# One-core adaptive-norm transformer block: last orthogonalisation moved ahead of one feed-forward batch, and the dense products of the block solve spread between the small ones

## The chip, the core and the metric

The program runs on one core of one Trainium2 chip. TensorE (PE) multiplies into eight PSUM banks, ScalarE (ACT) empties the banks, VectorE (DVE) does reductions and elementwise work, GpSimd (POOL) takes a few powers, SyncE (SP) issues the DMAs. The metric is the device time of one execution in microseconds; lower is better.

## The reference

For each of 16 batches of 512 tokens with 128 features: a modulated layer norm, then a chunked ridge attention with 16 heads of 64 features in four chunks of 128 tokens, then a second modulated layer norm and a feed-forward layer whose operands are rounded to a four-bit grid in blocks of 16.

```python
def step(S, qkv):
    Qc, Kc, Vc = qkv
    G = Kc.T @ Kc + RIDGE_EPS * I
    W = jnp.linalg.solve(G, Kc.T @ Vc)
    U = U0
    for _ in range(POWER_K):
        U, _ = jnp.linalg.qr(W @ U)
    Wr = U @ (U.T @ W)
    S_new = DECAY_ALPHA * S + Wr
    return (S_new, SCALE * (Qc @ S_new))
...
gate = fp4_linear(x, w_gate)
y = fp4_linear(x, w_up)
h = jax.nn.silu(gate) * y
return fp4_linear(h, w_down)
```

## The kernel before

The batches are taken in four groups (g = 0 to 3) of four. A group has 256 small systems of size 64 (16 chunks times 16 heads). Each 64x64 Gram matrix is inverted by halves of 32: `lead_extract` turns the leading 32x32 blocks so that VectorE can factor 256 of them at once (`factor`, called by `lead(g)`); `schur(g)` forms the Schur complement on TensorE, VectorE factors that too (`schur(g)` of the vector program), and `assemble(g)` puts the inverse together. `subspace(g)` then applies the inverses in the power iteration, VectorE orthogonalises the eight basis vectors (`orthogonalise(g)`), and `output(g)` and `write(g)` make the attention output.

TensorE's `schur` and `assemble` share one inner scheme, called **a solve stage** here. It runs over four parts k of 64 systems. `scale_rows(k)` is 64 small products (32x32 weights, 64 columns, line 697) into two banks. `squares(k)` takes four banks: first four dense products, called **masks** here (128x128 weights, 256 columns, line 707), which put the known half of the result into each bank, and then 64 small products (line 713) that add the squares of the scaled rows. The order is scale(0), scale(1), masks(0) and squares(0), scale(2), masks(1) and squares(1), scale(3), masks(2) and squares(2), masks(3) and squares(3). A float32 product is two matmul records in the profile, each with a weight load of its own, so one stage has 1056 matmul records: 1024 small and 32 dense.

All engines work in the order in which their instructions are written. TensorE and ScalarE run the same list of steps: a step of TensorE fills banks in turn, the same step of ScalarE empties them. `straight` runs steps one after another; `woven` interleaves two lists by the share of their banks that is done. A `yield` in a step is a place where `woven` may change lists.

In the main loop, for g = 0 to 2, the order on TensorE is assemble(g) (woven with write(g-1) where there is one), subspace(g), lead_return(g+1), schur(g+1), then output(g) woven with the next group's Gram stage. VectorE's order is schur(g), lead(g+1), one weight quantisation, orthogonalise(g), schur(g+1). schur(0) is woven with the fronts (the first layer norms) of batches 8 to 15.

The last group (`last_group`, line 1273) is woven with the feed-forward batches. A batch b has three steps on TensorE and ScalarE: `g` (transposes of the hidden input, then eight products with the gate and up weights), `t` (transposes of the quantised hidden layer) and `y` (down projection, residual). The list `steps` says in which order, `begin` and `wait` cut it: the steps up to `begin` are woven with subspace(3), those up to `wait` follow straight, the others up to batch 7 are woven with output(3) and write(3), which begins by waiting for VectorE's orthogonalise(3) (line 867). On VectorE `quantise(b)` stands between g(b) and t(b); it waits for ScalarE's flag `gate_ok`. ScalarE in turn empties g(b)'s products only when quantise(b-1) has read the ones before (line 953, `hh_ok`). `tile_hat(n)` (steps `n`) is ScalarE's normalisation of a group of four batches, `hidden.stats` and `hidden.finish` are VectorE's parts of the same.

Of the kernel before, what the change touches and what calls it, by code (L numbers as in the profile page):

```python
# [41 lines left out]
DH = 64  # L42
# [14 lines left out]
GB_N = 4  # L57
G = B // GB_N
T = GB_N * NC
HB = 32  # L60
# [222 lines left out]
NQ = T * HP  # L283
# [45 lines left out]
def main_pass(nc, x, ln_g, ln_b, c, wmod, Wq, Wk, Wv, Wo, w_gate, w_up, w_down, s_mod, s_c, s_xnt, s_base, s_x1, out):  # L329


    with ExitStack() as ctx:
# [145 lines left out]
        class Tensor:  # L478
# [211 lines left out]
            def scale_rows(self, k, stationary, moving):  # L690

                two = self.u.fill(2, apart=True)
                for i in range(8):
                    for c in range(4):
                        for s in range(2):
                            q = 32 * k + 8 * c + i
                            last = nc.tensor.matmul(two[s][HB * c:HB * c + HB, i * DH:(i + 1) * DH], stationary(s, q), moving(s, q),  # L697
                                                    start=True, stop=True)
                last.then_inc(filled, 2)
                return self.u.mark()  # L700

            def squares(self, k, half, mask, known):

                four = self.u.fill(4, apart=True)
                for c in range(4):
                    at = 32 * k + 8 * c
                    nc.tensor.matmul(four[c][:].rearrange("p (q z c) -> p q z c", z=2, c=HB)[:, :, half], mask[:], known[:, at:at + 8, :],  # L707
                                     start=True, stop=False, skip_group_check=True)
                for i in range(8):
                    for c in range(4):  # L710
                        for s in range(2):
                            both = scaled[HB * c:HB * c + HB, (2 * k + s) * 8 + i, :]
                            last = nc.tensor.matmul(four[c][rows(s, None), i * DH:(i + 1) * DH], both, both, start=False, stop=True,  # L713
                                                    skip_group_check=True)
                last.then_inc(filled, 4)
                return self.u.mark()

            def schur(self, g):
# [4 lines left out]

                def scale(k):
                    return self.scale_rows(k, lambda s, q: work[rows(s, 0), q, :],
                                           lambda s, q: beside(eyes[0][rows(s, 0)], gram[rows(s, 0), q, :]))

                marks = [scale(0)]
                yield
                for k in range(NQ // 32):  # L730
                    if k + 1 < NQ // 32:
                        marks.append(scale(k + 1))
                        yield
                    self.u.need(marks[k], apart=True)
                    m = self.squares(k, 1, minus[1], gram)
                    yield
                yield from self.to_problems(gram, m)

            def assemble(self, g):
# [6 lines left out]

                def scale(k):
                    return self.scale_rows(k, lambda s, q: work[rows(s, 1), q, :],
                                           lambda s, q: beside(kept[rows(s, 1), q, :], eyes[1][rows(s, 1)]))

                marks = [scale(0)]
                yield
                for k in range(NQ // 32):
                    if k + 1 < NQ // 32:
                        marks.append(scale(k + 1))
                        yield
                    self.u.need(marks[k], apart=True)
                    self.squares(k, 0, minus[0], kept)
                    yield
# [163 lines left out]
        class Scalar:  # L923
# [177 lines left out]
            def solved(self, dst, scale=1.0):  # L1101
                self.scale_rows(0)
                yield
                for k in range(NQ // 32):
                    if k + 1 < NQ // 32:
                        self.scale_rows(k + 1)
                        yield
# [656 lines left out]
```

## Time and profile before

| | us |
|---|---|
| median of three executions | 1335.05 (1333.93 to 1336.13) |
| the profiled execution | 1337.31 |
| its span, first to last instruction | 1335.5 |

| engine | busy us | share of the span | instructions |
|---|---|---|---|
| TensorE, matmul | 989.9 | 74% | 17632 |
| TensorE, weight load | 762.0 | 57% | 17632 |
| VectorE | 1118.0 | 84% | 3452 |
| ScalarE | 661.8 | 50% | 1392 |
| GpSimd | 174.6 | 13% | 118 |

The shares are means over stages with different limits. In the main loop VectorE's factorisations and TensorE's stages alternate in holding the chain; in the last third the feed-forward batches keep TensorE, ScalarE and VectorE busy together. The profile's chain of work that ended last is 54% TensorE, 31% VectorE, 9% ScalarE and 4% issue.

### The profile page before, as it was taken

The page shows a single profiled execution, that of the slowest core. Times are in us where ns is not written, and L with a number is a line of the kernel's source. Part 1 is how long each engine was busy: PE and PEld are TensorE (multiplying, and loading weights), DVE is VectorE, ACT ScalarE, POOL GpSimd, SP SyncE. Part 2 cuts the span into 40 slices and gives each one's busy share as a digit, 9 for nine tenths or more (in the row PEclk, how much of TensorE's full clock was granted, in tenths as well). Part 3 has the DMA queues.
Part 4 walks back from the last instruction along what each step waited for, and adds up shares of the span by engine and source line. Part 5 has one row for each costly group of instructions (what it writes and reads, how often), then busy time and mean ns, then how long its engine had stood idle before and what let it go on. Part 6 is the DMA issues. An engine that isn't in the chain of part 4 may idle for free.

```text
span 1335.5 us, 41205 instructions
## 1 busy us (share of the span) xinstructions
PE 989.9 (74%) x17632; PEld 762.0 (57%) x17632; DVE 1118.0 (84%) x3452; ACT 661.8 (50%) x1392; POOL 174.6 (13%) x118
## 2 busy tenths in 40 slices
PE   1693017596687899897899897782499838998597
PEld 0463016555576667776767777672477625765254
DVE  6875996699999599999599999689889699764996
ACT  3683017555344567645467645352246515655254
POOL 2420123201011001011001111001200020001000
PEclk9897558798688899899799899796699958999799
DMA  4321003300000001110002110013112100111001
GB/s 149 104 99 38 0 0 129 127 25 17 3 4 3 3 18 33 35 51 3 4 10 73 34 36 3 4 31 129 33 36 71 51 30 18 48 48 32 8 17 32
DMA packets 42693, 53.04 MB, mean 40 GB/s; under 512 B 2992, under 2 KB 25600, under 8 KB 42512
## 3 DMA queue, kind: packets, MB, share of 16 engines
q1 hardware_dynamic: 42512, 50.42, 11.4%
q8 instruction: 139, 2.28, 0.7%
q14 instruction: 42, 0.34, 0.1%
HBM read 32.53 MB, written 17.87 MB: 38 GB/s over the span
## 4 chain that ended last, share of the span: by engine, by line
PE 54%; DVE 31%; ACT 9%; issue 4%; POOL 1%; DMA 0%; DVEq 0%; ACTq 0%; POOLq 0%
PE a_bank L547 7%; PE a_bank L618 6%; PE a_bank L707 5%; DVE a_outer L1564 4%; DVE a_total L1570 4%; DVE a_outer L1568 4%; DVE a_blocks L1573 4%; PE a_bank L713 3%; PE a_bank L697 3%; PE a_bank L561 3%; PE a_bank L832 3%; PE a_bank L817 3%; PE a_bank L799 3%; PE a_bank L643 2%; PE a_bank L769 2%
## 5 line engine op out<-in xcount | busy, mean ns | idle before, releaser
L987 ACT ACTIVATE a_work<-a_bank 128x512 f32<-128x512 f32 (+1 forms) x193 | 109.3, 606 | 180.9 <-PE a_bank L675 138.5
L1487 POOL TENSOR_TENSOR a_root<-a_recip,a_half 128x32 f32<-128x32 f32 (+2 forms) x24 | 89.8, 3742 | 592.7 <-DVEq L1559 575.2
L675 PE MATMUL a_bank<-a_ident,a_blocks 128*128 128x128 f32 x256 | 38.5, 318 | 134.6 <-DVE a_blocks L1584 134.6
L1564 DVE TENSOR_TENSOR a_outer<-a_blocks,a_weight 128x62 f32<-128x62 f32 (+15 forms) x248 | 129.6, 523 | 0.0
L1570 DVE TENSOR_REDUCE a_total<-a_outer 128x62 f32<-128x62 f32 (+30 forms) x248 | 127.2, 513 | 0.3
L987 ACT ACTIVATE a_solve<-a_bank 128x512 f32<-128x512 f32 (+2 forms) x184 | 88.0, 526 | 69.2 <-PE a_bank L713 52.9
L1568 DVE TENSOR_TENSOR a_outer<-a_blocks 128x60 f32<-128x60 f32 (+14 forms) x240 | 119.4, 497 | 0.0
L1573 DVE TENSOR_TENSOR a_blocks<-a_blocks,a_outer 128x60 f32<-128x60 f32 (+14 forms) x240 | 118.6, 494 | 0.0
L675 PEld LDWEIGHTS a_bank<-a_ident,a_blocks 128*128 128x128 f32 x256 | 37.1, 203 | 135.5 <-DVE a_blocks L1584 135.5
L618 PE MATMUL a_bank<-a_scaled,a_blocks 128*128 128x352 f32 x256 | 92.6, 505 | 13.1 <-ACT a_blocks L987 13.1
L987 ACT ACTIVATE a_scaled<-a_bank 128x512 f32<-128x512 f32 (+2 forms) x133 | 66.8, 528 | 57.9 <-PE a_bank L697 46.2
L547 PE MATMUL a_bank<-a_wk,a_cg 128*128 128x512 f32 x192 | 90.4, 615 | 6.6 <-DMA a_cg<-s_c 6.6
L987 ACT ACTIVATE a_xb<-a_bank 128x512 f32<-128x512 f32 x108 | 64.3, 599 | 55.8 <-PE a_bank L817 23.6
L707 PE MATMUL a_bank<-a_solve,a_minus 128*128 128x256 f32 x256 | 87.3, 501 | 0.2 <-issue 0.2
L697 PE MATMUL a_bank<-a_solve,a_work 32*32 32x64 f32 x4096 | 54.8, 239 | 40.1 <-issue 30.8
L697 PEld LDWEIGHTS a_bank<-a_solve,a_work 32*32 32x32 f32 x4096 | 46.8, 111 | 46.5 <-issue 44.9
L618 PEld LDWEIGHTS a_bank<-a_scaled,a_blocks 128*128 128x128 f32 x256 | 49.3, 205 | 40.2 <-ACT a_blocks L987 16.2
L707 PEld LDWEIGHTS a_bank<-a_solve,a_minus 128*128 128x128 f32 x256 | 62.0, 254 | 12.8 <-issue 1.4
L817 PE MATMUL a_bank<-a_pair,a_yz 128*16 128x64 f32 x3072 | 54.3, 225 | 12.6 <-issue 5.9
L561 PE MATMUL a_bank<-a_work,a_wk 128*64 128x128 f32 x1024 | 62.1, 275 | 0.0
L561 PEld LDWEIGHTS a_bank<-a_work,a_wk 128*64 128x64 f32 x1024 | 55.4, 137 | 11.7 <-ACT a_work L987 8.3
L1012 ACT ACTIVATE a_pair<-a_pair,a_xa 128x128 f32<-128x128 f32 x128 | 51.6, 488 | 21.3 <-DVE a_xa L1639 21.3
(198 smaller groups left out, 2232.0 us busy)
## 6 DMA issues: line engine op xcount, KB each, us to landing
a_pair<-in_L_attn_x SPq DMA_DIRECT2D x16, 256.0 KB, 3.0
s_base<-a_pair SPq DMA_DIRECT2D x16, 256.0 KB, 2.8
s_xnt<-a_xb SPq DMA_DIRECT2D x12, 256.0 KB, 2.0
s_c<-a_xc SPq DMA_DIRECT2D x12, 256.0 KB, 2.6
a_cg<-s_c SPq DMA_DIRECT2D x12, 256.0 KB, 2.8
a_cc<-s_c SPq DMA_DIRECT2D x12, 256.0 KB, 3.4
a_blocks<-s_base SPq DMA_DIRECT2D x12, 256.0 KB, 3.4
s_x<-a_xc SPq DMA_DIRECT2D x12, 256.0 KB, 2.0
```

What stands on the lines that cost most here:

```text
L547: last = nc.tensor.matmul(bank[:], moment, wk[:, 8 * half:8 * half + 8, :].rearrange("p h d -> p (h d)"), start=True, stop=True)
L561: last = nc.tensor.matmul(bank[rows(s, None), i * P:(i + 1) * P].rearrange("p (t c) -> p t c", t=2), wk[:, h, :], ck[tp % 2][:, :, h * DH: ...
L618: last = nc.tensor.matmul(bank[:, 0:FI], ht[:, t], w_gu[:, i], start=True, stop=True)
L697: last = nc.tensor.matmul(two[s][HB * c:HB * c + HB, i * DH:(i + 1) * DH], stationary(s, q), moving(s, q), start=True, stop=True)
L707: nc.tensor.matmul(four[c][:].rearrange("p (q z c) -> p q z c", z=2, c=HB)[:, :, half], mask[:], known[:, at:at + 8, :], start=True, stop= ...
L817: last = nc.tensor.matmul(bank[32 * c:32 * c + 2 * R, i * DH:(i + 1) * DH], yz[:, q].rearrange("p z r -> p (z r)"), pair[:, q, :], start=T ...
L987: nc.scalar.activation(out, view, ACT.Copy, scale=scale).then_inc(emptied, 1)
L1487: nc.gpsimd.tensor_tensor(root[:, :, a:b], recip[:, :, a:b], half[:, :, a:b], ALU.pow).then_inc(roots_ok, 1)
L1564: known = ch.inc(V.tensor_tensor(terms, m[:, :, i:HB, 0:i], bcast(weight[:, :, 0:i], 2, n_i), ALU.mult))
L1568: product = ch.inc(V.tensor_tensor(step, bcast(m[:, :, j, i:HB], 2, j), bcast(row, 3, n_i), ALU.mult))
L1570: summed = ch.inc(V.tensor_reduce(total[:, :, 0:n_i], terms, op=ALU.add, axis=AX_X))
L1573: ch.inc(V.tensor_tensor(rest, rest, step, ALU.add))
```

## The change

There are two parts. First, the solve stage becomes one generator, `solved`: the masks of part k are no longer issued in front of squares(k) but one by one inside scale(k+1), one after every 16 small products; each takes its own bank with its own wait. The last part's masks stay together. scale(k+1) and squares(k) are no longer separated by a `yield`. Second, in the last group, `begin` and `wait` move and the step y(1) goes ahead of g(3): subspace(3) is woven with g(0), g(1), t(0), g(2), y(0); t(1) and y(1) follow straight; g(3), t(2) and all later steps are woven with output(3). On VectorE orthogonalise(3) stands ahead of quantise(2) instead of quantise(3), and `hidden.stats(2)`, `tile_hat(2)` and `hidden.finish(2)` each come one batch later.

```diff
-            def scale_rows(self, k, stationary, moving):
...
-            def squares(self, k, half, mask, known):
...
+            def solved(self, stationary, moving, half, mask, known):
...
+                def known_into(k, c):
+                    bank = self.u.fill(apart=True)
                     at = 32 * k + 8 * c
-                    nc.tensor.matmul(four[c][:].rearrange("p (q z c) -> p q z c", z=2, c=HB)[:, :, half], mask[:], known[:, at:at + 8, :],
+                    nc.tensor.matmul(bank[:].rearrange("p (q z c) -> p q z c", z=2, c=HB)[:, :, half], mask[:], known[:, at:at + 8, :],
                                      start=True, stop=False, skip_group_check=True)
...
+                def scale(k, before):
+                    two, four = self.u.fill(2, apart=True), []
+                    for i in range(8):
+                        for c in range(4):
+                            for s in range(2):
+                                q = 32 * k + 8 * c + i
+                                last = nc.tensor.matmul(two[s][HB * c:HB * c + HB, i * DH:(i + 1) * DH], stationary(s, q), moving(s, q),
+                                                        start=True, stop=True)
+                        if before is not None and i % 2 == 1 and i < 7:
+                            four.append(known_into(before, i // 2))
+                    last.then_inc(filled, 2)
+                    if before is not None:
+                        four.append(known_into(before, 3))
+                    return four
...
+                for k in range(parts):
+                    ready = mark
+                    if k + 1 < parts:
+                        mark = self.u.n + 2
+                        four = scale(k + 1, k)
+                    else:
+                        four = [known_into(k, c) for c in range(4)]
+                    self.u.need(ready, apart=True)
...
@@ ScalarE, solved @@
                     if k + 1 < NQ // 32:
                         self.scale_rows(k + 1)
-                        yield
                     self.squares(k, dst, scale)
                     yield
@@ last_group @@
-            for n, b in ((2, 2), (G - 1, EARLY - 4)):
+            for n, b in ((2, 3), (G - 1, EARLY - 4)):
                 steps.insert(steps.index(("y", b)) + 1, ("n", n))
-            begin = steps.index(("y", 1)) + 1
-            wait = steps.index(("t", 2)) + 1
+            at = steps.index(("g", 3))
+            steps[at:at + 2] = [("y", 1), ("g", 3)]
+            begin = steps.index(("y", 0)) + 1
+            wait = steps.index(("y", 1)) + 1
@@ VectorE, batches @@
-                    if b == GB_N - 1:
+                    if b == 2:
                         orthogonalise(G - 1)
+                    if b == GB_N:
                         hidden.stats(dve, ch, 2, 4, hx[0], passed)
-                    if b == GB_N + 1:
+                    if b == GB_N + 2:
                         dve.wait_ge(hidden.hat_ok, 1)
                         hidden.finish(ch, 2)
```

How the instructions stand on TensorE in schur(1), before. The names are output <- operands, `a_bank` is a PSUM bank, and the last number is how many such products follow one another.

```order
L675 MATMUL a_bank<-a_ident,a_blocks 128x128 x32
L697 MATMUL a_bank<-a_solve,a_work 32x64 x128
L707 MATMUL a_bank<-a_solve,a_minus 128x8x32 x4
L713 MATMUL a_bank<-a_scaled 64x64 x64
L697 MATMUL a_bank<-a_solve,a_work 32x64 x64
L707 MATMUL a_bank<-a_solve,a_minus 128x8x32 x4
L713 MATMUL a_bank<-a_scaled 64x64 x64
```

The same place with the change (line 708 is the scaling, 698 the mask, 732 the squares):

```order
L675 MATMUL a_bank<-a_ident,a_blocks 128x128 x32
L708 MATMUL a_bank<-a_solve,a_work 32x64 x80
L698 MATMUL a_bank<-a_solve,a_minus 128x8x32
L708 MATMUL a_bank<-a_solve,a_work 32x64 x16
L698 MATMUL a_bank<-a_solve,a_minus 128x8x32
L708 MATMUL a_bank<-a_solve,a_work 32x64 x16
L698 MATMUL a_bank<-a_solve,a_minus 128x8x32
L708 MATMUL a_bank<-a_solve,a_work 32x64 x16
L698 MATMUL a_bank<-a_solve,a_minus 128x8x32
L732 MATMUL a_bank<-a_scaled 64x64 x64
```

The four masks in a row have become four single ones with 16 small products between, and the squares follow the last of them.

TensorE at the end of subspace(3) and the start of output(3), before. Line 832 is subspace's second half of the inverse, 618 and 608 are a step g, 860 the turn of the basis (out of `a_yb` at the end of subspace, out of `a_basis` at the start of output), 643 to 653 a step y, 631 a step t.

```order
L618 MATMUL a_bank<-a_scaled,a_blocks 128x352 x2
L860 MATMUL a_bank<-a_ident,a_yb 128x128 x8
L643 MATMUL a_bank<-a_solve,a_work 128x512 x3
L650 MATMUL a_bank<-a_blocks,a_ident 128x512
L653 MATMUL a_bank<-a_ident,a_turned_out 128x128 x4
L631 MATMUL a_bank<-a_ident,a_work 128x128 x8
L631 MATMUL a_bank<-a_ident,a_work 96x128 x4
L860 MATMUL a_bank<-a_ident,a_basis 128x128 x8
```

With the change (line 856 was 860, 828 was 832):

```order
L618 MATMUL a_bank<-a_scaled,a_blocks 128x352 x2
L828 MATMUL a_bank<-a_ident,a_xa 64x32 x16
L856 MATMUL a_bank<-a_ident,a_yb 128x128 x8
L643 MATMUL a_bank<-a_solve,a_work 128x512 x3
L650 MATMUL a_bank<-a_blocks,a_ident 128x512
L653 MATMUL a_bank<-a_ident,a_turned_out 128x128 x4
L631 MATMUL a_bank<-a_ident,a_work 128x128 x8
L631 MATMUL a_bank<-a_ident,a_work 96x128 x4
L643 MATMUL a_bank<-a_solve,a_work 128x512 x3
L650 MATMUL a_bank<-a_blocks,a_ident 128x512
L653 MATMUL a_bank<-a_ident,a_turned_out 128x128 x4
L856 MATMUL a_bank<-a_ident,a_basis 128x128 x8
```

Before, y(1) and t(2) stand between the two turns; now y(0), t(1) and y(1) do, and the last step of subspace follows its predecessor (828) with no step of a batch in between.

## Rows read from the trace of the kernel before

**Rows 1.** Who waited for whom: VectorE; total us, times, longest.
```profile
DVE a_blocks L1552 <- ACTq L992: 58.7, 7, 13.7
```

**Rows 2.** Busy time by stretch, the solve stages of schur(1), schur(2), schur(3).
```profile
core 0: us, PE busy (x) PEld busy (x) DVE busy (x) ACT busy (x) POOL busy (x), PEclk, DMA share, GB/s
424.42:453.92 29.50, 24.52 (x1056) 19.86 (x1056) 23.14 (x50) 10.43 (x20) 3.28 (x2) 0.83 0.02 4
627.02:658.50 31.48, 27.27 (x1056) 21.98 (x1056) 22.98 (x49) 10.54 (x20) 3.28 (x2) 0.73 0.02 4
833.20:865.00 31.80, 26.75 (x1056) 21.68 (x1056) 22.88 (x49) 10.54 (x20) 3.28 (x2) 0.73 0.02 4
```

**Rows 3.** TensorE in order of time, schur(2): start, us, instruction, idle before.
```profile
627.02 2.05 PE L697 MATMUL a_bank<-a_solve,a_work 32*32 32x64 f32 x185 [1.48 <-ACT a_work L987]
631.00 1.32 PE L697 MATMUL a_bank<-a_solve,a_work 32*32 32x64 f32 x71 [1.93 <-issue]
632.25 3.78 PE L707 MATMUL a_bank<-a_solve,a_minus 128*128 128x256 f32 x8
635.96 2.10 PE L713 MATMUL a_bank<-a_scaled 32*64 32x64 f32 x128
637.99 0.72 PE L697 MATMUL a_bank<-a_solve,a_work 32*32 32x64 f32 x48
639.80 1.03 PE L697 MATMUL a_bank<-a_solve,a_work 32*32 32x64 f32 x80 [1.09 <-issue]
```

**Rows 4.** DMA of 627 to 660 us in 40 slices, and its instruction queue.
```profile
GB/s 0 20 0 0 0 0 20 0 0 0 0 0 20 0 0 0 20 0 0 0 0 0 20 0 0 0 20 0 0 0 0 10 20 0 0 0 0 20 0 0
...
q8 instruction: 8, 0.13, 1.4%
```

**Rows 5.** TensorE in order of time, schur(1), masks at full clock.
```profile
444.90 1.96 PE L707 MATMUL a_bank<-a_solve,a_minus 128*128 128x256 f32 x8
```

**Rows 6.** Groups of instructions by line, schur(2): busy us, mean ns.
```profile
L707 PEld LDWEIGHTS a_bank<-a_solve,a_minus 128*128 128x128 f32 x32 | 8.9, 291 | 2.3 <-issue 0.3
L713 PE MATMUL a_bank<-a_scaled 32*64 32x64 f32 x512 | 7.4, 267 | 0.0
```

**Rows 7.** TensorE in order of time, end of subspace(1), start of lead_return(2).
```profile
620.79 1.16 PE L860 MATMUL a_bank<-a_ident,a_yb 128*128 128x128 f32 x8 [0.48 <-ACT a_yb L987]
621.79 1.39 PE L675 MATMUL a_bank<-a_ident,a_blocks 128*128 128x128 f32 x11
```

**Rows 8.** Busy time by stretch: subspace(3) woven, then output(3) and write(3) woven.
```profile
1000.10:1058.50 58.40, 58.39 (x1002) 43.78 (x1003) 46.54 (x59) 37.34 (x77) 0.00 (x0) 1.00 0.17 56
1118.20:1214.00 95.80, 91.71 (x710) 64.44 (x711) 62.77 (x78) 54.38 (x115) 0.00 (x0) 0.98 0.11 34
```

**Rows 9.** Chain of waits, subspace(3): start, us on the chain, what.
```profile
1038.02 2.77 PE a_bank L643 x6
...
1041.81 1.06 PE a_bank L650 x2
1042.87 0.89 PE a_bank L653 x8
...
1044.82 1.46 PE a_bank L631 x12
...
1047.29 0.59 PE a_bank L608 x4
...
1048.93 1.38 PE a_bank L618 x4
```

**Rows 10.** VectorE in order of time: quantise(0), quantise(1), orthogonalise(3) begin.
```profile
1014.13 1.63 DVE L1619 TENSOR_TENSOR a_work<-a_scaled 128x1408 f32<-128x1408 f32 x1 [1.26 <-ACTq L992]
...
1025.45 1.62 DVE L1619 TENSOR_TENSOR a_work<-a_scaled 128x1408 f32<-128x1408 f32 x1
...
1059.36 1.23 DVE L1602 TENSOR_TENSOR a_outer<-a_basis 128x1024 f32<-128x1024 f32 x1 [10.30 <-ACTq L992]
```

**Rows 11.** TensorE in order of time, first instruction of output(3).
```profile
1089.51 1.97 PE L860 MATMUL a_bank<-a_ident,a_basis 128*128 128x128 f32 x8 [24.10 <-DVE a_basis L1614]
```

**Rows 12.** DMA issues: KB each, us to landing (`hidden.load_x`).
```profile
a_solve<-s_x SPq DMA_DIRECT2D x3, 1024.0 KB, 7.8
```

More of the change, by code:

```diff
@@ L688, in lead_return @@
                 self.at["lead"] = self.u.mark()
-            def scale_rows(self, k, stationary, moving):
[L692 to L700, printed above, removed]
@@ L702, in squares @@
-            def squares(self, k, half, mask, known):
-                four = self.u.fill(4, apart=True)
-                for c in range(4):
+            def solved(self, stationary, moving, half, mask, known):
+                parts = NQ // 32
+                def known_into(k, c):
+                    bank = self.u.fill(apart=True)
                     at = 32 * k + 8 * c
-                    nc.tensor.matmul(four[c][:].rearrange("p (q z c) -> p q z c", z=2, c=HB)[:, :, half], mask[:], known[:, at:at + 8, :],
+                    nc.tensor.matmul(bank[:].rearrange("p (q z c) -> p q z c", z=2, c=HB)[:, :, half], mask[:], known[:, at:at + 8, :],
@@ L708, in squares @@
                                      start=True, stop=False, skip_group_check=True)
[L709 to L714, printed above, removed]
@@ L715, in squares @@
-                last.then_inc(filled, 4)
+                    return bank
+                def scale(k, before):
[12 more added lines that the diff above has]
+                    return four
@@ new lines, in solved @@
+                mark = self.u.n + 2
+                scale(0, None)
+                yield
+                for k in range(parts):
+                    ready = mark
+                    if k + 1 < parts:
+                        mark = self.u.n + 2
+                        four = scale(k + 1, k)
+                    else:
+                        four = [known_into(k, c) for c in range(4)]
+                    self.u.need(ready, apart=True)
+                    for i in range(8):
+                        for c in range(4):
+                            for s in range(2):
+                                both = scaled[HB * c:HB * c + HB, (2 * k + s) * 8 + i, :]
+                                last = nc.tensor.matmul(four[c][rows(s, None), i * DH:(i + 1) * DH], both, both, start=False, stop=True,
+                                                        skip_group_check=True)
+                    last.then_inc(filled, 4)
+                    yield
@@ L722, in schur @@
                 self.u.need(self.at["lead"], apart=True)
[L724 to L728, printed above, removed]
-                yield
[L730 to L736, printed above, removed]
+                m = yield from self.solved(lambda s, q: work[rows(s, 0), q, :], lambda s, q: beside(eyes[0][rows(s, 0)], gram[rows(s, 0), q, :]),
+                                           1, minus[1], gram)
                 yield from self.to_problems(gram, m)
@@ L745, in assemble @@
                 self.pe.sem_inc(schur_read, 1)
[L747 to L759, printed above, removed]
+                yield from self.solved(lambda s, q: work[rows(s, 1), q, :], lambda s, q: beside(kept[rows(s, 1), q, :], eyes[1][rows(s, 1)]),
+                                       0, minus[0], kept)
             def moments(self, src, mark):
@@ L1106, in solved @@
                         self.scale_rows(k + 1)
-                        yield
                     self.squares(k, dst, scale)
```

## The prediction, made before the change was run

> **What bounds the kernel now.** I began with the view of who waited for whom. VectorE, the busiest engine, stands idle 58.7 us in front of seven of its eight factorisations, 13.7 at the longest [rows 1]: TensorE and ScalarE must first hand it the next blocks. In the main loop the work between orthogonalise(g) and the next factorisation is lead_return, the solve stage of schur and the turn back, on TensorE alone. So a microsecond saved in schur(1), schur(2) or schur(3) is a microsecond of the program.
>
> The view by stretches gives these stages 29.50, 31.48 and 31.80 us, of which TensorE's matmuls are busy 24.5 to 27.3, at a mean granted clock of 0.83, 0.73 and 0.73 [rows 2]. As the clock has two levels, 1.0 (2.4 GHz) and 0.5 (1.2 GHz), it is at the lower one for 34%, 54% and 54% of the time.
>
> The view in order of time shows why [rows 3]. After 185 small records TensorE stops for 1.93 us with nothing to wait for ("issue"); then come 71 + 8 + 128 + 48 = 255 records and the next such stop, 1.09 us. The DMA view of the same 33 us has 8 packets of the instruction queue [rows 4] for 1056 records, one for some 130. I read this as code that arrives in blocks of about 128 records, of which two are held: a block that is used up faster than the next one lands ends in a stop. The packets are never closer than four of the 40 slices, 4 x 0.825 = 3.3 us [rows 4], so a block costs the larger of 3.3 us and its own work. 128 small records at full clock are 128 x 2.05/185 = 1.4 us of work [rows 3]. After each stop the clock is low and the four masks take 3.78 us [rows 3] instead of 1.96 [rows 5]. Blocks of small products alone and blocks with a slow run of masks thus take turns: both are dear.
>
> In the last group TensorE is the bound: busy 58.39 of 58.40 us in subspace(3) with its batches, 91.71 of 95.80 in most of the weave with output(3) [rows 8]. Between the two it stands 24.1 us for orthogonalise(3) [rows 11], which had itself waited 10.3 us for subspace(3) [rows 10].
>
> **Part 1, the solve stage.** No product is added or removed. Of the 16 masks of a stage, 12 move between small products and 4, the last part's, stay together. Added are three bank waits in each of three parts. The banks that they ask for were last filled by squares(k-1) and by the scaling before it; ScalarE empties these while scale(k+1) begins, so I cost the waits at nothing. Were ScalarE late, the squares queued behind the mask would be late by as much.
>
> A block in the new order holds one mask and 126 small records, or three masks and 122. At full clock a mask is 1.96/4 = 0.49 us [rows 5], first switch included. One-mask block: 126 x 0.0111 + 0.49 = 1.9, so 3.3 by the code. Three masks: 1.35 + 1.47 = 2.8, with some 0.15 a mask for changing between small and dense (below) 3.3. In schur(2), from the end of the first stop (631.00) to 658.50, there are 871 records in 27.5 us [rows 2, 3]. New: six blocks of 3.3 and 103 small records, 19.8 + 1.2 = 21.0: 6.5 us saved. schur(3) is 0.3 longer before, 6.8; schur(1) is 2.0 shorter and its first stop ends half a microsecond earlier, about 4.8. That is 18 in all, the upper end.
>
> The lower end is the low clock throughout: 71 records took 1.32 us, 18 ns each, and a mask 3.78/4 = 0.95 [rows 3]. One mask: 2.3 + 0.95 + 0.15 = 3.4; three: 2.2 + 2.85 + 0.45 = 5.5; three such pairs and the rest 28.6 against 27.5. Summed over the three stages that is a loss of about 5.
>
> The new stops are 3.3 minus 1.9 or less, so shorter than the 1.93 after which the clock fell, and dense work stands in every block. I take the lower level for a third of the time, schur(1)'s share now. Each third costs a third of 18 + 5 = 23, so part 1 gives 18 - 7.7 = **10 us** (-5 to 18).
>
> A rule that speaks against it: the Trainium skill, TensorEngine Tiling (Array Packing), section Key Properties, says that changing the tiling mode drains TensorE, and the change makes 24 more such switches in a stage. In the trace masks behind small products take 1.96 us and eight records at 0.43 a mask would be 1.7, so a switch shows as 0.2 us or less. The Trainium skill, Runtime: NRT & Kernel Launch, section Instruction fetch mechanics, has the blocks of 256 instructions that I infer, but calls the refill mostly hidden; the stops in the rows say that here it is not, and by that rule part 1 would give nothing.
>
> The other solve stages: assemble(1), (2) and (3) are woven with write, whose dense products already let the code catch up; the straight assemble(0) runs under VectorE's lead(1). What they save passes on, since lead_return(2) began with no wait right behind subspace(1) [rows 7]. A shorter first stop there is offset in part: three of write's running sums now follow one another directly, each waiting for ScalarE to empty the one before. I take 1 us for the three (-3 to 4). schur(0) is woven with fronts that VectorE and ScalarE pace: 1 us (-1 to 3).
>
> **Part 2, the last group.** Out of the stretch that leads to orthogonalise(3) go t(1), 1.46 us, g(3), 0.59 + 4 x 1.38 = 6.1, and y(0), 2.77 + 1.06 + 0.89 = 4.7 [rows 9]: 12.3, all TensorE time. With fewer steps of batches between, three steps of subspace now directly follow the one whose result they need, 0.48 us each [rows 7]: 1.4. So orthogonalise(3) begins 10.9 us earlier, near 1048.5.
>
> VectorE must be free by then. g(0) is also stretched out: its products end some 17.8 us after 1000.1 instead of 13.4 (sums of the same row kinds), so quantise(0) begins near 1018.6 instead of 1014.1; a batch takes 1025.45 - 1014.13 = 11.3 us [rows 10], so quantise(1) ends near 1041. t(0) is reached near 1031, as quantise(0) ends at 1030: about 1 us of slack.
>
> The removed work comes back. g(3) and t(2) now lie in the weave with output(3), which TensorE bounds: 6.1 + 1.5 = 7.6. y(0) and t(1) fill the wait for orthogonalise(3) beside y(1). Net 10.9 - 7.6 = **3.3 us** (-1 to 6). Behind it: quantise(2) starts when orthogonalise(3) ends, and t(2), behind eight products of g(3) and the first output steps, comes later than its 11.3 us. ScalarE raises `hidden.used` only with g(3), so SyncE's load for batches 8 to 11 starts some 30 us later; its 7.8 us [rows 12] lie under quantise(2) and quantise(3), 22.6 us. tile_hat(2), finish(2) and the stats move by one batch with their readers.
>
> **Sum.** 10 + 1 + 1 + 3.3 = 15.3 from the profiled 1337.3 gives 1322.0; that execution lies 2.3 above the median of 1335.05, so the time is near **1320**.
>
> **Rivals.** *The stops or the low clock stay* (19%): the code still paces every block and the masks run slow, part 1 between -5 and 0; with 3 from part 2, 1332 to 1339. For it: the lower level follows each stop. Against: masks right behind small products do run at full clock where no stop came just before [rows 5]. *Part 2 gives nothing* (13%): t(0) waits for the later quantise(0), or other steps of subspace lose their cover; 1323 to 1328. *All at full clock* (10%): part 1 gives 18, about 1310.
>
> *Slower* (8%): each mask between small products drains the array, so that a small product's 267 ns and the mask's load of 291 ns [rows 6] are exposed, 0.56 us a mask instead of 0.15. It is paid 12 times in each of the three schur and three assemble stages on the path, 72 x 0.41 = 30 us: near 1350. It decides from 0.15 + 15.3/72 = 0.36 us a mask.
>
> *The forecast* (50%): 1311 to 1328.
>
> The range leaves out half of the full-clock case and nearly all of the slower ones: 1308 to 1336. A measurement tells 0.2%, 2.7 us, from no change. Faster: forecast, part 2 empty, full clock, and 5 of the 19 points of the first rival, 78%; the same, 9 of these; slower, the other 5 and the drain, 13%.
>
> **What would show it.** In the profile after, schur(1) to (3) should take 25 to 28 us, the longest issue stop there stay under 1.5 us, and VectorE's idle time before the factorisations fall from 58.7 to about 47. orthogonalise(3) should begin about 11 us earlier than the rest of the program has moved, TensorE's wait for it fall from 24 to about 18, and t(0) not wait for VectorE. A stage of 30 us or more, or masks of 0.9 us throughout, refutes part 1; a shift of orthogonalise(3) of less than 8 us refutes part 2.

## The result, and the profile after

The change makes the kernel slower: 1365.6 us median of four runs (1360.0 to 1370.7) beside 1335.6 for the kernel before in the same comparison, ratio 1.022 (95% interval 1.017 to 1.027). A second comparison (e8_changed_again, below) gave 1.0286 (1.025 to 1.032). The forecast was 1320 us, faster. The profiled run took 1366.75 us, span 1364.9, which is 29.4 us more than the span before.

Who waited for whom, VectorE, after (total us, times, longest). The idle time ahead of the factorisations, 58.7 before [rows 1], should have fallen to 47; it rose:

```profile
DVE a_blocks L1549 <- ACTq L988: 71.4, 7, 17.9
```

Busy time by stretch, schur(1), schur(2) and schur(3) after; they answer to [rows 2]. Each is 3.9 to 4.3 us longer, 12.1 in all, and the granted clock has fallen from 0.83, 0.73, 0.73:

```profile
core 0: us, PE busy (x) PEld busy (x) DVE busy (x) ACT busy (x) POOL busy (x), PEclk, DMA share, GB/s
426.65:460.07 33.42, 29.55 (x1056) 20.26 (x1056) 23.29 (x50) 10.54 (x20) 3.28 (x2) 0.74 0.02 4
639.23:674.97 35.74, 33.01 (x1056) 21.86 (x1056) 22.99 (x49) 10.54 (x20) 3.28 (x2) 0.62 0.02 4
854.54:890.25 35.71, 32.71 (x1056) 21.82 (x1056) 22.98 (x49) 10.54 (x20) 3.28 (x2) 0.62 0.02 4
```

The same view of the other stages, assemble(1) to (3) woven with write, first before, then after:

```profile
547.47:585.13 37.66, 34.80 (x1133) 28.40 (x1133) 36.62 (x111) 16.08 (x31) 5.43 (x1) 0.91 0.15 52
752.03:792.71 40.68, 35.77 (x1133) 28.80 (x1133) 39.58 (x119) 16.03 (x31) 5.43 (x1) 0.87 0.14 49
957.92:997.06 39.14, 35.33 (x1133) 28.65 (x1133) 34.67 (x78) 16.08 (x31) 3.19 (x2) 0.91 0.15 51
```

```profile
553.51:597.86 44.35, 39.20 (x1133) 27.95 (x1133) 43.11 (x132) 15.99 (x31) 5.43 (x1) 0.88 0.13 45
768.46:812.93 44.47, 38.86 (x1133) 27.75 (x1133) 43.23 (x132) 16.01 (x31) 5.43 (x1) 0.88 0.13 44
984.30:1028.32 44.02, 38.08 (x1133) 27.36 (x1133) 39.15 (x81) 16.02 (x31) 3.46 (x3) 0.92 0.14 45
```

Here 6.7, 3.8 and 4.9 are lost, 15.4 us, where the forecast had a gain of 1. The first factorisation behind schur(0) starts 2.3 us later, at 264.1 instead of 261.7, and from the start of subspace(3) to the end the run takes 333.5 us instead of 335.4. With these the sum is 28 of the 29.4. The 2.3 us are not clear of chance: in e2, e12 and e11 below, which leave schur(0) as it was, that factorisation starts at 255.6, 255.6 and 261.0.

TensorE in order of time in schur(2) after, which answers to [rows 3] (line 708 is the scaling, 698 the masks, two records each, 732 the squares):

```profile
639.23 1.78 PE L708 MATMUL a_bank<-a_solve,a_work 32*32 32x64 f32 x160 [1.47 <-ACT a_work L983]
...
642.77 0.63 PE L698 MATMUL a_bank<-a_solve,a_minus 128*128 128x256 f32 x1 [1.35 <-issue]
643.34 0.68 PE L708 MATMUL a_bank<-a_solve,a_work 32*32 32x64 f32 x32
643.95 1.22 PE L698 MATMUL a_bank<-a_solve,a_minus 128*128 128x256 f32 x2
645.10 0.68 PE L708 MATMUL a_bank<-a_solve,a_work 32*32 32x64 f32 x32
...
652.00 0.44 PE L708 MATMUL a_bank<-a_solve,a_work 32*32 32x64 f32 x10 [0.54 <-issue]
...
670.35 1.99 PE L698 MATMUL a_bank<-a_solve,a_minus 128*128 128x256 f32 x8
...
674.61 0.35 PE L732 MATMUL a_bank<-a_scaled 32*64 32x64 f32 x10 [0.83 <-issue]
```

And the stretch from the first stop to the last four masks, then the rest, by the view of stretches (same columns as above):

```profile
643.00:670.00 27.00, 26.46 (x753) 16.62 (x757) 19.38 (x44) 7.38 (x14) 3.28 (x2) 0.50 0.02 4
670.40:674.90 4.50, 3.67 (x138) 2.96 (x136) 0.00 (x0) 2.06 (x4) 0.00 (x0) 1.00 0.02 4
```

The third stop of the same stage before, behind the two in [rows 3]:

```profile
647.72 1.55 PE L697 MATMUL a_bank<-a_solve,a_work 32*32 32x64 f32 x90 [1.18 <-issue]
```

The stops did shrink, from 1.93 + 1.09 + 1.18 to 1.35 + 0.54 + 0.83. But TensorE worked for 27 us with half a microsecond of rest and its clock stood at 0.50 throughout; it was at 1.00 again in the stretch that begins with the four masks that the change had left together. It rose just as they began (0.50 up to 670.2 us, 0.79 from there to 670.4), and the four took 1.99 us, as at full clock, so these rows alone don't show that the four masks raised it. At 0.50, sixteen small products and one mask take 645.10 - 643.34 = 1.76 us. At full clock, in assemble(1), the same unit takes 570.98 - 569.96 = 1.02:

```profile
569.96 0.45 PE L708 MATMUL a_bank<-a_solve,a_work 32*32 32x64 f32 x32
570.35 0.70 PE L698 MATMUL a_bank<-a_solve,a_minus 128*128 128x256 f32 x2
570.98 0.45 PE L708 MATMUL a_bank<-a_solve,a_work 32*32 32x64 f32 x32
```

The last group did roughly what was forecast. TensorE at the start of output(3), and VectorE at the start of orthogonalise(3):

```profile
1112.08 1.97 PE L856 MATMUL a_bank<-a_ident,a_basis 128*128 128x128 f32 x8 [18.38 <-DVE a_basis L1611]
```

```profile
1081.94 1.22 DVE L1599 TENSOR_TENSOR a_outer<-a_basis 128x1024 f32<-128x1024 f32 x1 [8.84 <-ACTq L988]
```

subspace(3) begins at 1031.36 after and at 1000.10 before, so orthogonalise(3) begins 50.6 us behind it instead of 59.3 [rows 10], and the wait has fallen from 24.1 [rows 11] to 18.4.

### The profile page after: what moved, and what is told of

It reads as the page before. It is cut to its first block, busy times and chain, and to the rows that moved or that the text cites. A ratio compares the mean times of both kernels' runs of the same rounds, so it can differ in the third digit from the quotient of the medians.

```text
span 1364.9 us, 41301 instructions
## 1 busy us (share of the span) xinstructions
PE 1019.8 (75%) x17632; PEld 755.2 (55%) x17632; DVE 1118.3 (82%) x3452; ACT 663.0 (49%) x1392; POOL 174.6 (13%) x118
## 4 chain that ended last, share of the span: by engine, by line
PE 54%; DVE 30%; ACT 10%; issue 4%; DMA 1%; POOL 1%; SPq 0%; DVEq 0%; ACTq 0%; POOLq 0%
PE a_bank L547 6%; PE a_bank L698 6%; PE a_bank L618 6%; DVE a_outer L1561 4%; DVE a_total L1567 4%; PE a_bank L732 4%; PE a_bank L708 4%; DVE a_outer L1565 4%; DVE a_blocks L1570 4%; PE a_bank L561 3%; PE a_bank L828 3%; PE a_bank L813 3%; PE a_bank L795 2%; PE a_bank L664 2%; PE a_bank L765 2%
## 5 line engine op out<-in xcount | busy, mean ns | idle before, releaser
L698 PE MATMUL a_bank<-a_solve,a_minus 128*128 128x256 f32 x256 | 108.7, 531 | 5.1 <-issue 3.8
L708 PE MATMUL a_bank<-a_solve,a_work 32*32 32x64 f32 x4096 | 66.2, 247 | 20.6 <-issue 11.3
L732 PEld LDWEIGHTS a_bank<-a_scaled 32*64 32x64 f32 x4096 | 56.2, 160 | 22.2 <-issue 22.2
L732 PE MATMUL a_bank<-a_scaled 32*64 32x64 f32 x4096 | 62.8, 268 | 5.5 <-issue 5.4
L698 PEld LDWEIGHTS a_bank<-a_solve,a_minus 128*128 128x128 f32 x256 | 51.3, 239 | 20.0 <-issue 12.2
```

What stands on the lines that cost most here:

```text
L698: nc.tensor.matmul(bank[:].rearrange("p (q z c) -> p q z c", z=2, c=HB)[:, :, half], mask[:], known[:, at:at + 8, :], start=True, stop=Fal ...
```

## The theories and the experiments

**S**, the switch: each further run of masks between small products costs TensorE a fixed time. **C**, the clock: masks one at a time leave the clock low, four together bring it back. **Y**, the weave: without the pause (`yield`) between scaling and masks, write's steps can't stand there. **W**, the bank waits that the change adds. S, the prediction's last rival, was priced anew from the trace after: four masks and 64 small products apart from each other take 1.82 + 1.40 = 3.22 us at full clock (second block of rows under e5), four units 4 x 1.02 = 4.08, so 0.29 for each of the three further runs of a part, nine a stage. All ratios are against the kernel before on the same chip.

| run | what it is | median us | ratio (95%) |
|---|---|---|---|
| e2_part2, e12_part2_again | part 2 alone | 1329.5, 1323.9 | 0.9972 (0.995 to 0.999), 0.9958 (0.993 to 0.998) |
| e1_part1 | part 1 alone | 1373.3 | 1.0316 (1.028 to 1.035) |
| e8_changed_again | both | 1366.3 | 1.0286 (1.025 to 1.032) |
| e6_waits | e2 and scattered waits | 1336.6 | 1.0046 (1.002 to 1.007) |
| e5_no_yields | e2 without pauses | 1342.6 | 1.0097 (1.006 to 1.013) |
| e3_together | e2, waits and no pauses, masks by fours | 1348.7 | 1.0125 (1.010 to 1.015) |
| e4_pairs | the same as e3, masks by twos | 1360.5 | 1.0207 (1.018 to 1.024) |
| e9_halves | the change with half masks | 1391.2 | 1.0456 (1.041 to 1.050) |
| e7_twice | the change, each mask twice | 1379.2 | 1.0359 (1.031 to 1.041) |
| e10_schur_only | e2, single masks in schur alone | 1341.9 | 1.0090 (1.006 to 1.012) |
| e11_write_ahead | e2, write's steps one earlier | 1316.9 | 0.9898 (0.986 to 0.994) |

**e1_part1** takes the diff without its hunks in `last_group` and in VectorE's list of batches; **e2_part2** takes those alone.

> The solve stages of the changed kernel with the last group of the kernel before. In the changed kernel's profile the three schur and three assemble stages on the path are 12.1 and 15.4 us longer than before, schur(0) costs 2.3, and the last group gains 1.8. If the stages carry the whole loss, this run is 1.8 us above the changed kernel, near 1367 us. If the two parts work on each other (the shifted start of the last group), it lies at 1360 or less.

> The solve stages of the kernel before with the last group of the changed kernel. Reading of the trace: orthogonalise(3) starts 8.7 us earlier after the start of subspace(3), and the tail 1.8 us earlier, so 1333.5 us here, a ratio of 0.9987. Rival, that the 1.8 us come from part 1's delay in the assemble stage just ahead, with writes already done: 1335 or more. What the prediction said of part 2: 1332.

> The changed kernel once more, beside the kernels of this call: 1.022 as first measured. e1_part1, which has part 1 alone, gave 1.0316, and part 2 alone gave 0.9972, so if the two parts only add, this is 1.0288; at 1.022 part 2 is worth more (9 us) behind part 1 than alone (3.6 us).

> e2_part2 again, as the base of e10_schur_only and e11_write_ahead on the same chip: 0.9972 (0.995 to 0.999).

Part 1 carries the whole loss. Part 2 gains 3.6 and 7.0 us in its two comparisons. 1.0316 x 0.9972 = 1.0287 is what e8_changed_again measured, so the parts add. The first measurement of the change, 1.022, is lower; the intervals overlap.

**e3_together** and **e4_pairs** keep the changed kernel's waits and leave the pauses out, but issue the masks in runs of four and of two. The cut below is e3's; e4 issues two masks behind 32 and two behind 64 small products.

```diff
                         if before is not None and i % 2 == 1 and i < 7:
-                            four.append(known_into(before, i // 2))
+                            four.append(self.u.fill(apart=True))
                     last.then_inc(filled, 2)
                     if before is not None:
-                        four.append(known_into(before, 3))
+                        four.append(self.u.fill(apart=True))
+                        for c in range(4):
+                            known_into(before, c, four[c])
...
-                        four = [known_into(k, c) for c in range(4)]
+                        four = [self.u.fill(apart=True) for c in range(4)]
+                        for c in range(4):
+                            known_into(k, c, four[c])
```

> The changed kernel with every bank wait where it is, after each 16 small products, and no interleaving steps at the yields that it dropped; only the four masks of a part are issued together behind its 64 small products. Theory S (each further run of masks between small products costs 0.29 us at either clock, 9 further runs in a stage): the six stages on the path give back 16 us, 1350 us. Theory S with C (with single masks the clock also stays low, 0.62 in schur(2) and (3) against 0.73): schur(1) to (3) return to 29 to 32 us and the three assemble stages give back about 8, 1340 to 1345; what is left over before is the weave without its yields (theory Y, 7 us in the three assemble stages). Theory W (the added bank waits are what costs): no change from 1366.

> The changed kernel with two runs of two masks a part, after 32 and 64 small products, instead of four runs of one; waits unchanged. Theory S alone: 6 of 9 further runs of a stage go, two thirds of 16 us, so 1355. With C in proportion to the length of a run: schur(2) and (3) between 31.5 and 35.7 us at a clock between 0.62 and 0.73, about 1350. If the clock rises behind a pair as it does behind four, as before: 1345. Theory W: 1366.

In e3_together schur(1) to (3) took 30.9, 33.8 and 32.0 us at clocks of 0.83, 0.75 and 0.84. The 33.8 hold a wait of 2.5 us for ScalarE ahead of the last four masks that the changed kernel doesn't have there: in e3 and e4 these four ask for all their banks before the first is issued. The assemble stages gave back only 2.9 us in all of the 8 expected, so most of their loss isn't the masks' place. W is refuted as the main cause. In e4_pairs schur(2) and (3) took 33.9 (with such a wait of 2.5) and 33.2 at 0.70 and 0.74, between the two as C in proportion has it, but the assemble stages took 44.3, 47.4 and 44.7, no less than in the changed kernel, and the whole, 1360, lies above every value expected under S or C: two runs of two cost 11 us more than one of four, and four runs of one 2 to 11 more again.

**e5_no_yields** and **e6_waits** split what is left:

```diff
@@ e5: schur and assemble on TensorE; the same line on ScalarE @@
                         marks.append(scale(k + 1))
-                        yield
@@ e6: scale_rows, behind each i @@
+                    if k and i in (1, 3, 5):
+                        self.u.need(self.u.n - RING, apart=True)
```

> e2_part2 with one edit: the pause between the scaling of part k+1 and the masks of part k is dropped on TensorE and ScalarE, so that the other part of a weave can't put a step there; no wait added, masks four together. It splits the 19 us (1.4%) that lie between e2_part2 (0.9972) and e3_together (1.0125). Theory Y (the weave: write's running sums follow one another and wait for ScalarE): schur(1) to (3), which stand alone, as in e2_part2, 30 to 32 us; the three assemble stages 2 to 5 us longer each, ratio 1.004 to 1.010. If the pauses carry all: 1.0125. If the scattered bank waits carry all (theory W): 0.997.

> e2_part2 with three bank waits that are already met put behind the 16th, 32nd and 48th small product of parts 1 to 3, where the changed kernel has them; pauses and masks as before. Theory W: each such wait ahead of small products costs some 0.2 us or brings one more stop, 9 a stage, schur(1) to (3) 2 us longer each, all six stages 11 to 13 us, ratio 1.006 or more. Theory Y: waits that are met cost nothing, 0.997.

e5 agrees with Y, at its upper end: the pauses alone cost 1.25% against e2, 17 us, and the value for pauses that carry all, 1.0125, lies within the interval too. In its profile schur(1) to (3) took 31.0, 29.6 and 30.1, no longer than in e2 (31.1, 32.1, 29.7), and the assemble stages 45.1, 45.0 and 42.1 against 40.7, 40.5 and 39.3, 11.6 us more. TensorE in order of time in assemble(2), first e5 (line 697 scaling, 707 masks, 885 and 899 steps of write), then e2, where write's lines are 887, 901, 896, 916, 918:

```profile
760.70 0.68 PE L697 MATMUL a_bank<-a_solve,a_work 32*32 32x64 f32 x31 [2.90 <-issue]
761.31 3.78 PE L707 MATMUL a_bank<-a_solve,a_minus 128*128 128x256 f32 x8
765.02 2.02 PE L713 MATMUL a_bank<-a_scaled 32*64 32x64 f32 x128
766.98 1.09 PE L885 MATMUL a_bank<-a_ident,a_xa 128*128 128x128 f32 x8
770.18 2.07 PE L899 MATMUL a_bank<-a_xa,a_xc 128*128 128x128 f32 x8 [2.11 <-ACT a_xa L985]
772.18 2.04 PE L697 MATMUL a_bank<-a_solve,a_work 32*32 32x64 f32 x128
774.16 3.18 PE L707 MATMUL a_bank<-a_solve,a_minus 128*128 128x256 f32 x8
```

```profile
760.62 0.68 PE L697 MATMUL a_bank<-a_solve,a_work 32*32 32x64 f32 x31 [2.73 <-issue]
761.23 1.97 PE L887 MATMUL a_bank<-a_ident,a_xa 128*128 128x128 f32 x8
762.99 2.62 PE L707 MATMUL a_bank<-a_solve,a_minus 128*128 128x256 f32 x8
...
773.83 2.32 PE L707 MATMUL a_bank<-a_solve,a_minus 128*128 128x256 f32 x8
...
782.27 1.48 PE L697 MATMUL a_bank<-a_solve,a_work 32*32 32x64 f32 x128
783.67 1.12 PE L916 MATMUL a_bank<-a_blocks,a_ident 128*128 128x512 f32 x2
...
785.53 1.89 PE L707 MATMUL a_bank<-a_solve,a_minus 128*128 128x256 f32 x8
787.35 0.87 PE L713 MATMUL a_bank<-a_scaled 32*64 32x64 f32 x62
```

With the pause, write's transposes stand between the small products and the masks. Without it the masks follow the stop at the lower clock (3.78 us for 2.62, then 3.18 for 2.32), and write's first running sum comes right behind the transposes that it needs and waits 2.11 us for ScalarE, where e2 shows no wait. In each of the three stages TensorE waits at least 2.8 us more for ScalarE than in e2: 2.1 for this sum and 0.7 for a later one. That is 8.4 of the 11.6 us; about 3 are left for the clock, which is 0.85, 0.81 and 0.92 against 0.87, 0.87 and 0.91 in e2, and for the stops.

e6 stays open. Its ratio is 0.7% above e2's, but its profile has every stage as long as in e2 (schur 30.5, 31.7, 30.2, assemble 39.0, 39.5, 39.5), so the rows don't show where the 7 us between the medians would go. The two profiled executions are only 1.7 us apart (1334.0 and 1332.3), so the kept traces don't hold most of that difference. In e3, where the same waits are added to e5, they make 0.3%, within the uncertainty.

**e9_halves** doubles the switches and **e7_twice** the dense work:

```diff
@@ e9: a mask of 4 systems, 128 columns, for z = 0 and then z = 1, 8 small products apart @@
-                    at = 32 * k + 8 * c
+                    at = 32 * k + 8 * c + 4 * z
@@ e7: known_into @@
+                    for n in range(2):
                         nc.tensor.matmul(bank[:].rearrange("p (q z c) -> p q z c", z=2, c=HB)[:, :, half], mask[:], known[:, at:at + 8, :],
                                          start=True, stop=False, skip_group_check=True)
```

> The changed kernel with every mask cut into two of 128 columns, the first half behind 16, 32 and 48 small products as before, the second behind 8 more; the last mask of a part stays whole in place. The dense columns and the waits stay the same, 9 more runs a stage. Theory S: 9 x 0.29 = 2.6 us a stage at whatever clock, 16 us in the six stages and 2 in schur(0), ratio 1.035 to 1.040 against the 1.022 and 1.0286 of the changed kernel. Theory C alone: the clock in schur(2) and (3) is at the lower level for most of the stage already (0.57 to 0.62) and falls further only in the assemble stages, 1.027 to 1.033; the time of 16 small products and a mask at one clock is the same as in the changed kernel, 1.02 us at full and 1.76 at the lower one. By S that time grows by 0.29.

> The changed kernel with every mask issued twice in a row into the same bank, 16 more dense products a stage, no further run. Theory S without C (the clock doesn't hang on how the masks lie): 16 x 0.43 us at full clock and 16 x 0.92 at the lower one come on top, so schur(2) and (3), 35.7 us at a clock of 0.62 in the changed kernel, take 42 to 48 us and the whole 1366 + 7 x 7 to 11 = 1415 to 1440. Theory C (too little dense work between the small products keeps the clock low): the clock in schur(2) and (3) rises to 0.8 or more, and in spite of the added products they take only 29 to 36 us; the whole 1385 to 1405.

TensorE in order of time in e9's assemble(1) (line 706 scaling, 697 half masks), at the lower clock and then at full:

```profile
574.32 0.46 PE L706 MATMUL a_bank<-a_solve,a_work 32*32 32x64 f32 x16
...
575.44 0.46 PE L706 MATMUL a_bank<-a_solve,a_work 32*32 32x64 f32 x16
...
580.32 1.22 PE L697 MATMUL a_bank<-a_solve,a_minus 128*128 128x128 f32 x4
...
592.13 0.34 PE L706 MATMUL a_bank<-a_solve,a_work 32*32 32x64 f32 x16
...
592.82 0.34 PE L706 MATMUL a_bank<-a_solve,a_work 32*32 32x64 f32 x16
...
595.85 0.71 PE L697 MATMUL a_bank<-a_solve,a_minus 128*128 128x128 f32 x4
```

Two such half units take 2 x 1.12 = 2.24 us at the lower clock and 2 x 0.69 = 1.38 at full, against 1.76 and 1.02 for 16 products and a whole mask. So a further run costs 0.48 and 0.36 us. A half mask also has weight loads of its own, which is a rival, but the last mask of a part settles it: its halves stand one behind the other (the two rows of four records) and take 1.22 and 0.71 us, as the whole mask does in the changed kernel (1.22 and 0.70). More loads without a further run cost nothing there. S is there at either clock, and dearer than the 0.29 expected.

The whole, 1.0456, lies above what S or C alone had, and the stages don't follow S alone. The three assemble stages took 52.7, 53.0 and 50.6 us at 0.77, 0.77 and 0.80, 6.5 to 8.5 more than in the changed kernel (0.88, 0.88, 0.92), where nine runs at 0.36 to 0.48 make 3.2 to 4.3: the clock fell too. schur(1) to (3) took 33.9, 36.6 and 36.7 us at 0.80, 0.72 and 0.58, only 0.5 to 1.0 more. In schur(3) TensorE is busy 3.8 us longer, as S has it, but its idle time falls from 3.0 to 0.1; in schur(1) and (2) the clock was higher than in the changed kernel.

Busy time by stretch, schur(1) to (3) of e7:

```profile
427.78:460.33 32.55, 30.51 (x1088) 23.05 (x1088) 22.97 (x49) 10.54 (x20) 3.28 (x2) 0.95 0.02 4
644.61:681.43 36.82, 34.48 (x1088) 24.99 (x1088) 22.98 (x49) 10.54 (x20) 3.29 (x2) 0.81 0.01 4
868.03:902.53 34.50, 32.63 (x1088) 24.03 (x1088) 22.98 (x49) 10.54 (x20) 3.29 (x2) 0.90 0.02 4
```

Sixteen masks more, at least 16 x 0.455 = 7.3 us at full clock (1.82/4 each), and the stages take 0.9 less, 1.1 more and 1.2 less than in the changed kernel: the clock rose from 0.74, 0.62, 0.62 to 0.95, 0.81, 0.90. That is C, and S without C (42 us or more) is refuted. The whole, 1379, is below even C's 1385.

**e10_schur_only** has the changed kernel's `solved` for schur and the old stage, pauses included, for assemble.

> e2_part2 with single masks between the small products in schur alone; the four assemble stages, weave and pauses included, as before. It is the prediction's largest term by itself (10 us gained, -5 to 18, so 0.990). Theory S without C: 2.6 us more a stage, 1.5 to 2 us of stops less, so about 3 to 5 us over the four stages, 1.000. Theory S with C: schur(1) to (3) as in the changed kernel, 33 to 36 us at a clock of 0.57 to 0.75, and schur(0) 2 us longer, 14 us together: 1.0077.

```profile
423.49:457.06 33.57, 29.07 (x1056) 19.79 (x1056) 23.24 (x50) 10.54 (x20) 3.28 (x2) 0.75 0.02 4
632.91:666.55 33.64, 31.36 (x1056) 21.31 (x1056) 22.96 (x49) 10.54 (x20) 3.28 (x2) 0.64 0.02 4
839.09:872.16 33.07, 32.34 (x1056) 21.59 (x1056) 22.97 (x49) 10.54 (x20) 3.28 (x2) 0.59 0.02 4
```

These rows, schur(1) to (3) by stretch, are S with C. In schur(3) TensorE is busy 32.34 of 33.07 us: hardly a stop is left, and the stage is still longer than in e12 on the same chip (31.6 us at 0.73). The three stages are 9.9 us longer than in e12, and VectorE's idle time ahead of the factorisations is 65.6 us against 54.3. Single masks in schur alone cost 1.2 to 1.3% against e2 and e12, 16 to 18 us. With the pauses' 1.25% that is 2.5 of the 3.1 to 3.3% by which the change lies above part 2 alone; the rest, 8 to 11 us, is left for the single masks in the assemble stages and for the waits, which no run separates.

**e11_write_ahead** turns the finding on the weave round. The order of write (0) and assemble (1) is written out, with each of write's steps from the fourth on one place earlier:

```diff
-            woven(e, (e.write(g - 1), WRITE_UNITS), (e.assemble(g), ASSEMBLE_UNITS))
+            woven(e, (e.write(g - 1), WRITE_UNITS), (e.assemble(g), ASSEMBLE_UNITS), by="011011010101010101010010")
```

> A version that may beat both: e2_part2 with the order of write's and assemble's steps written out, so that write's last step of transposes stands between the first two scalings (256 small products in a row before, with a stop of 2.6 to 2.9 us in them) and each of the four running sums has a step of assemble ahead of it (the third and fourth followed one another with a wait of 0.7 us). Dense work in those 256 products hides 0.9 us of the stop, and the wait of 0.7 goes: about 1.6 us a stage, 5 in all, 0.9935. If a shorter stop keeps the clock up: 2 to 3 us more a stage, 0.988. Rival: the first running sum, now right behind the second scaling, waits for ScalarE, which has to empty four banks first, 1 to 2 us a stage: 0.998 to 1.000.

Busy time by stretch, assemble(1) to (3), and TensorE in order of time at the start of assemble(1):

```profile
547.63:581.85 34.22, 32.51 (x1133) 26.49 (x1133) 33.27 (x102) 15.82 (x30) 5.24 (x1) 1.00 0.17 58
747.51:785.26 37.75, 36.26 (x1133) 29.22 (x1133) 36.72 (x112) 15.91 (x31) 5.43 (x1) 0.86 0.16 52
950.76:985.34 34.58, 32.82 (x1133) 26.65 (x1133) 30.00 (x70) 15.91 (x31) 3.34 (x3) 1.00 0.18 57
```

```profile
547.63 1.46 PE L697 MATMUL a_bank<-a_solve,a_work 32*32 32x64 f32 x128 [1.62 <-ACT a_xa L987]
549.03 1.09 PE L887 MATMUL a_bank<-a_ident,a_xa 128*128 128x128 f32 x8
...
552.64 0.82 PE L697 MATMUL a_bank<-a_solve,a_work 32*32 32x64 f32 x60 [1.71 <-issue]
```

With one step of transposes among the 256 small products the stop is 1.71 us here, where e2 and e12 have 2.3 to 2.9, and the waits of 0.7 us for ScalarE are gone. In assemble(1) and (3) the clock then never falls: 34.2 and 34.6 us where e12, on the same chip, took 39.7 and 39.7. In assemble(2) the clock is 0.86 and the stage 37.8 (38.3 in e12). There the clock fell at 749.5 us, among the transposes and 2.3 us ahead of a stop of only 1.49, so the length of this stop doesn't decide it. This version beats both kernels: 1316.9 us, 1.0% below the kernel before, between the two values expected. Part 2 carries 0.4 of it (e12), the new order the other 0.6, 7 us, though the two intervals just overlap; from the start of schur(1) to that of subspace(3) the profiles take 564.7 us and 576.

## Why the prediction was wrong, step by step

**The bound was right.** The three schur stages grew by 12.1 us and VectorE's idle time ahead of its factorisations by 12.7. A microsecond there is one of the program.

**Part 1, schur: 10 us forecast as gain, 12.1 lost.** The stops shrank: over the three stages TensorE's idle time (length less busy time) fell from 14.2 to 9.6 us, though schur(1) has stops of 1.84 and 1.69, above the 1.5 that I had named. Its busy time rose by 16.7, which leaves the 12.1. The step that failed is "I take the lower level for a third of the time": it was 52%, 76% and 76% (clocks of 0.74, 0.62, 0.62). I had argued that a stop shorter than 1.93 us wouldn't bring the clock down and that a dense product in every block would hold it up. After a stop of 1.35 it was down all the same, and it stayed down for 27 us of masks one at a time; with runs of four and nearly the same waits (e3) the stages were at 0.83, 0.75 and 0.84.

The lower end of the range, a loss of 5, was itself reckoned too small. Three pairs of blocks hold 12 masks, but the 871 records hold 15, since only one was issued before and the last part's four come too. The three left out, at 0.95 us less two small records of 18 ns each, are 2.7 us a stage and 8 in all, so the lower end is a loss of 13. With it and the measured two thirds at the lower level, the forecast's own sum gives a loss of 3, where 12.1 were measured.

A further step is the price of a further run, "some 0.15 a mask": four units against four masks and 128 small records apart are 4.08 against 3.22 us at full clock and 7.04 against 5.69 at the lower one (1.76 x 4; 3.71 + 1.98 in e5's rows), so 0.21 and 0.34 for each of the twelve masks. In schur(2), 4.3 us longer, three parts of 1.35 make 4.1, the stops give back 1.5, and 1.7 remain; I put them down to the longer time at the lower clock, by difference and not by a measurement.

**The first rival (19%)**, that the low clock stays, had the mechanism of the schur stages right. Its price, part 1 between -5 and 0, came from that lower end.

**The drain rival (8%)** had the right sign and place, and too high a price: 0.56 a mask, deciding from 0.36. At 0.21 to 0.34 over 72 masks it takes 15 to 24 us. That is less than the deciding price and still a loss, since the gain that it had to outweigh didn't come. The change makes nine further runs in a stage, so 18 further switches and not 24. The rule that I weighed against it, the Trainium skill, TensorEngine Tiling (Array Packing), Key Properties, says that a change of tiling mode drains TensorE. e9 agrees in sign; the runs give the price of a further run, 0.36 and 0.48 us, and don't show whether it is the drain. Against it I had set four masks behind small products, where one switch is shared by four and hard to see.

**The assemble stages: 1 us forecast as gain (-3 to 4), 15.4 lost.** The step is "A shorter first stop there is offset in part: three of write's running sums now follow one another directly". I named the waits that the dropped pauses bring and set them off against a gain; e5 has the pauses at 11.6 us by stages and 17 by the medians, and 8.4 of the 11.6 are waits for ScalarE. What I missed is that write's transposes, too, lose their place between scaling and masks: the first sum now comes right behind the last of them and waits 2.1 us, and the masks run at the lower clock for longer.

**schur(0)**: 1 us forecast as gain; the first factorisation behind it starts 2.3 us later, within the spread of the profiles. **Part 2**: 3.3 us forecast, 3.6 and 7.0 measured alone; from the start of subspace(3) to the end the profiles take 335.4 us before, 329.0 in e12 and 333.5 after. orthogonalise(3) moved by 8.7 us instead of 10.9, and TensorE's wait fell to 18.4 as forecast. What the forecast didn't have is that the products of the steps g wait longer for ScalarE, 22.0 us in all after and 22.2 in e2 against 13.1 before and in e1, with two stops of 6.5 and 6.8.

Open: 9 of the 12.1 us in schur, for which the dearer runs (36 masks at 0.06 to 0.19 above the 0.15, 2 to 7 us) are a part; what the scattered waits cost (e6); and why e11's assemble(2) lost its clock where assemble(1) and (3) kept it.

## What to carry to other kernels

Price a reordering on an engine whose clock moves by the granted clock of each stretch, and by what stands between the dense runs, not by stops alone: fewer stops and a busier engine came with a longer stage. In this kernel it paid to keep dense products in runs, and to use other dense work, not single products, to break up long runs of small ones. A place where a weave may change lists is work too: before dropping one, list what stood there and what it covered.

## What the runs showed that I had not expected

Twice the dense work in schur(1) to (3) left the stages within 1.2 us of their length, because the clock rose (e7). Write's steps moved one place ahead, the first of them between two runs of 128 small records, were worth 5.5 and 5.1 us in two stages of 40 (e11 against e12) and 0.6 in the third. And in the changed kernel's first four runs the time follows the mean clock: 0.868, 0.861, 0.854 and 0.849 gave 1360.0, 1364.4, 1366.8 and 1370.7 us. In the six runs of e8 it follows only loosely: 0.851 gave 1364.9 and 0.857 gave 1376.6.
